# Twelve feed-forward products become eleven, and the shared rotary key moves to the router's product

## What is computed

```python
# feed-forward of each of the two windowed layers, HID = 682
h = layernorm(shift_token(x)) @ w1 + b1          # 256 -> 2 x 682
a, g = split(h, 2)
x = x + (a * gelu(g)) @ w2 + b2                  # 682 -> 256

# latent attention: 16 heads of 16 + 8 rotary columns
c_kv = x @ W_DKV                                 # 256 -> 64
k    = concat(c_kv @ W_UK, rope(x @ W_KR))       # rotary key (8 columns) shared by all heads
# expert layer
logits = x @ gate_w                              # 256 -> 8
```

## Time and profile before

| what | value |
|---|---|
| median of 3 runs | 3233.68 us (3232.84 to 3268.52) |
| the profiled execution | 3231.55 us, its span 3229.8 us |
| PE busy | 2873.4 us, 89% of the span |
| DVE, ACT, POOL busy | 1565.0, 1166.9, 1066.9 us |
| mean granted clock of PE | 0.944 of full speed |
| first block ends, expert block begins | about 2606 us |
| length of a stage with retention, with latent attention | 143.3 us, 167.2 us |

### The profile page before, as it was taken

How to read it: one execution, slowest core, us unless ns; L and a number is a source line. 1 busy time by engine, 2 the same in 40 slices (tenths; PEclk the granted TensorE clock), 3 DMA queues, 4 the chain that set the end, 5 groups by cost and what they waited for, 6 DMA issues and landing times. The chain is left out here.

```text
span 3229.8 us, 41719 instructions
## 1 busy us (share of the span) xinstructions
PE 2873.4 (89%) x15902; PEld 1893.9 (59%) x15902; DVE 1565.0 (48%) x2994; ACT 1166.9 (36%) x2240; POOL 1066.9 (33%) x770
## 2 busy tenths in 40 slices
PE   6999899999989899898999899999988759999990
PEld 3565656556565655545554555555554349989990
DVE  5645456565545556475656565666654410000002
ACT  3444343434343344343444444444432212222221
POOL 4423233342323234252535344443432311111112
PEclk8999999999999999899999999999998679999995
DMA  3000000000001011001010101010101069998874
GB/s 126 10 20 17 24 26 24 14 24 20 17 23 48 21 50 45 14 4 46 4 46 4 47 4 46 4 46 4 40 4 40 2 230 351 349 339 328 324 296 159
DMA packets 86048, 261.69 MB, mean 81 GB/s; under 512 B 10940, under 2 KB 50188, under 8 KB 67164
## 3 DMA queue, kind: packets, MB, share of 16 engines
q1 hardware_dynamic: 79372, 241.26, 20.6%
q0 software_dynamic: 6480, 17.77, 1.4%
HBM read 210.69 MB, written 44.12 MB: 79 GB/s over the span
## 5 line engine op out<-in xcount | busy, mean ns | idle before, releaser
L1171 POOL TENSOR_TENSOR s_qk<-s_qk,s_rrec 128x1024 f32<-128x1024 f32 (+1 forms) x128 | 215.1, 1681 | 761.4 <-DVE s_rrec L1317 761.3
L547 PE MATMUL s_pA<-s_w_wqkv,s_curT 128*128 128x512 f32 x768 | 372.3, 624 | 5.8 <-ACT s_curT L932 3.9
L960 ACT ACTIVATE s_qk<-s_pA,s_mx 128x256 f32<-128x256 f32 (+1 forms) x512 | 221.5, 448 | 420.2 <-DVE s_mx L1313 420.1
L1843 PEld LDWEIGHTS m_ph<-m_xT,m_w 128*128 128x128 f32 x2272 | 267.4, 194 | 5.4 <-issue 1.8
L1843 PE MATMUL m_ph<-m_xT,m_w 128*128 128x128 f32 x2272 | 268.0, 277 | 1.2 <-DVE m_xT L1913 1.2
L1913 DVE COPY m_xT<-m_px 128x256 f32<-128x256 f32 x71 | 30.1, 424 | 476.3 <-PE m_px L1832 476.3
L1857 PE MATMUL m_py<-m_w,m_hT 128*128 128x256 f32 x1136 | 258.1, 381 | 0.0
L547 PEld LDWEIGHTS s_pA<-s_w_wqkv,s_curT 128*128 128x128 f32 x768 | 146.9, 198 | 183.0 <-issue 169.8
L1406 DVE TENSOR_SCALAR s_pairs<-s_pD 128x1024 f32<-128x1024 f32 (+1 forms) x192 | 193.7, 1038 | 105.6 <-PE s_pD L693 67.9
L693 PE MATMUL s_pD<-s_mixer 32*128 32x512 f32 (+3 forms) x1024 | 201.5, 511 | 47.3 <-DVE s_pairs L1406 38.0
L1857 PEld LDWEIGHTS m_py<-m_w,m_hT 128*128 128x128 f32 x1136 | 211.4, 191 | 26.1
(11 more groups left out here) (222 smaller groups left out, 5104.6 us busy)
## 6 DMA issues: line engine op xcount, KB each, us to landing
m_w<-in_m_w SPq DMA_DIRECT2D x142, 1024.0 KB, 5.7
m_xin<-rows_s SPq DMA_DIRECT2D x71, 129.0 KB
m_acc<-acc_s SPq DMA_DIRECT2D x16, 512.0 KB, 5.1
s_cur<-in_x SPq DMA_DIRECT2D x8, 512.0 KB, 3.4
xn_s<-s_cur SPq DMA_DIRECT2D x8, 512.0 KB, 2.6
s_s_tm<-xn_s SPq DMA_DIRECT2D x8, 512.0 KB, 3.2
cur_s<-s_cur SPq DMA_DIRECT2D x8, 512.0 KB, 2.6
s_s<-s_s_tm SPq DMA_DIRECT2D x8, 512.0 KB, 2.6
```

The source lines that it names most:

```text
L547: last = nc.tensor.matmul(out, lhs(c), rhs(c), start=(c == 0), stop=(c == n - 1))
L960: last = nc.scalar.activation(prob[u % 3][:, i * 256 + lo:(i + 1) * 256], ps[:, i * 256 + lo:(i + 1) * 256], ACT.Exp, bias=mx[:, u, i:i + ...
L1171: nc.gpsimd.tensor_tensor(pi, pi, rrec[:, u, :].unsqueeze(2).broadcast_to((P, 4, 256 - lo)), ALU.mult).then_inc(p_rdy, 1)
L1843: last = nc.tensor.matmul(ph[u % 2][:, f * P:(f + 1) * P], w1[:, u % NW, c * F + f * P:c * F + (f + 1) * P], xT[:, u % 2, c * P:(c + 1) * ...
```

## The change

In the feed-forward the chunks are 128 wide, five of them, and the sixth holds what is left, 42 columns. The weights `w1` are laid out anew: chunk by chunk, a then g, and in the last chunk both halves side by side, a at column 0 and g at column 64. So the last chunk is one product of 106 columns in ring D; ACT takes its gelu from ring D's bank (with a semaphore of its own, `last_gelu`), and DVE takes a from the same bank. The memset of the ones waits for this gelu.

For the shared key, the 8 key columns ride with the router's 8 in one product by token (`gw`, 16 columns), which moves ahead of the latent product. DVE rotates them by token with a small table (`lrot`), writes them into `krow` at four heads' places, and PE turns `krow` by four 128x128 transposes in unit 5, behind the value products; DVE copies the result into `KrT`. The product `kr` in its two sets goes, with its weights `lWkr`. POOL clears `krow` once, in stage 8, ahead of its memset of `Vaug`. On DVE the order of unit 4 is now key turn, logits, latents.

```diff
-HCH = 120
+HCH = 128
+LAST_G = 64
+UPW = 2 * HCH * (NHC - 1) + LAST_G + HSZ[-1]
@@ ring_a_jobs
-            if s.here:
+            if s.here and c < NHC - 1:
                 j += [("g", k, c)]
@@ ring_d_jobs
             if s.lat and u == 4:
-                j += [("lat", b), ("kr", b), ("rt", b)]
+                j += [("rt", b), ("lat", b)]
             if s.lat and u == 5:
-                j += head(b, 0)
+                j += [("kr", b)] + head(b, 0)
-WIDE = ("qkT", "S", "qk", "PT", "kr", "lq", "sc", "AT", "ro")
+WIDE = ("qkT", "S", "qk", "PT", "lq", "sc", "AT", "ro")
@@ SP
                 if k == B - 1:
-                    sp.wait_ge(outA, doneA["g", k, NHC - 1])
+                    sp.wait_ge(outA, doneA["g", k, NHC - 2])
@@ PE, up_projection
+                at = 2 * HCH * c
+                if c < NHC - 1:
+                    ps = slotA("g", b, c)
+                    project(ps, lambda k: W["w1"][:, k, at + HCH:at + 2 * HCH], lambda k: zT[:, k, :], DC).then_inc(mmA, 1)
                 ps = slotD("a", b, c)
-                project(ps[0:n, 0:T], lambda k: W["w1"][:, k, c * HCH:c * HCH + n], lambda k: zT[:, k, :], DC).then_inc(mmD, 1)
+                n = HCH if c < NHC - 1 else LAST_G + HSZ[c]
+                project(ps[0:n, 0:T], lambda k: W["w1"][:, k, at:at + n], lambda k: zT[:, k, :], DC).then_inc(mmD, 1)
@@ PE, latent_projections
+                ps = slotD("rt", b)
+                for t in range(NT):
+                    last = project(ps[:, t * (E + LDR):(t + 1) * (E + LDR)], lambda c: x1T[:, c, tile_cols(t)], lambda c: W["gw"][:, c, :], DC)
+                last.then_inc(mmD, 1)
                 ps = slotD("lat", b)
                 project(ps[:, 0:T], lambda c: W["lWd"][:, c, :], xT, DC).then_inc(mmD, 1)
+            def shared_key(b):
+                pe.wait_ge(krow_rdy, b + 1)
                 ps = slotD("kr", b)
-                for i in range(2):
-                    last = project(ps[:, i * T:(i + 1) * T], lambda c: W["lWkr"][:, i, c, :], xT, DC)
-                last.then_inc(mmD, 1)
-                ps = slotD("rt", b)
                 for t in range(NT):
-                    last = project(ps[:, t * E:(t + 1) * E], lambda c: x1T[:, c, tile_cols(t)], lambda c: W["gw"][:, c, :], DC)
+                    last = nc.tensor.transpose(ps[:, tile_cols(t)], krow[:, t].rearrange("p h d -> p (h d)"), ident[:])
                 last.then_inc(mmD, 1)
@@ PE, unit 5
                         latent_values_in(b)
+                        shared_key(b)
                         keys_queries(b, 0)
@@ ACT, gelu
+                at = 0 if c < NHC - 1 else LAST_G
+                if c < NHC - 1:
+                    ps = takeA("g", b, c)
+                else:
+                    act.wait_ge(mmD, DJ["a", b, c] + 1)
+                    ps = pD[:, colsD[DJ["a", b, c]]]
@@ POOL, stage 8
+                        nc.gpsimd.memset(krow, 0.0)
                         nc.gpsimd.memset(Vaug, 0.0).then_inc(vaug_rdy, 1)
@@ DVE, gate_up
-                dve.wait_ge(outA, doneA["g", b, c])
-                if c == NHC - 1:
-                    step(nc.vector.memset(hT[NHC - 1][64:HCH], 1.0))
+                if c < NHC - 1:
+                    dve.wait_ge(outA, doneA["g", b, c])
+                else:
+                    dve.wait_ge(last_gelu, b + 1)
+                    step(nc.vector.memset(hT[NHC - 1][32:64], 1.0))
@@ DVE, key turn (called by router_logits)
+                nc.vector.tensor_tensor(ktmp[:, 0], kr, W["lrot"][:, 0], ALU.mult)
+                for i in range(2):
+                    last = nc.vector.tensor_tensor(turned[:, :, :, i], pairs[:, :, :, 1 - i], sines[:, :, :, i], ALU.mult)
+                step(last)
+                if b == 0:
+                    dve.wait_ge(vaug_rdy, 2)
+                nc.vector.tensor_tensor(krow[:, :, :, LDH:LDH + LDR], ktmp[:, 0].unsqueeze(2).broadcast_to((P, NT, 4, LDR)),
+                                        ktmp[:, 1].unsqueeze(2).broadcast_to((P, NT, 4, LDR)), ALU.add).then_inc(krow_rdy, 1)
@@ DVE, shared_key
-                nc.vector.tensor_tensor(rm[:, 0, :], ps[:, 0:T], W["lcos"], ALU.mult)
-                nc.vector.tensor_tensor(rm[:, 1, :], ps[:, T:2 * T], W["lsin"], ALU.mult).then_inc(outD, 1)
-                dve.wait_ge(outD, doneD["kr", b])
-                step(nc.vector.tensor_tensor(KrT, rm[:, 0, :], rm[:, 1, :], ALU.add))
+                nc.vector.tensor_copy(KrT, ps).then_inc(outD, 1)
@@ DVE, units 4 and 5
                     if s.lat and u == 4:
+                        router_logits(b)
                         latent_in(b)
+                    if s.lat and u == 5:
                         shared_key(b)
-                        router_logits(b)
-                    if s.lat and u == 5:
                         keys_queries(b, 0)
```

More of the change, by code:

```diff
@@ L269, in stream_layers @@
         W["lWqk"] = part(mixer, 9480, 1024, i=2, g=LG, n=P)
-        W["lWkr"] = part(mixer, 10504, 512, i=2, c=DC, n=P)
+        krow = part(mixer, 10504, 512, t=NT, h=4, d=32)
         W["lWo"] = part(mixer, 11016, 512, c=DC, n=D)
@@ L273, in stream_layers @@
         W["lsin"] = part(mixer, 12040, 512)
-        W["gw"] = part(mixer, 12552, 16, c=DC, e=E)
+        W["gw"] = part(mixer, 12552, 32, c=DC, e=E + LDR)
+        W["lrot"] = part(mixer, 12584, 64, i=2, t=NT, d=LDR)
         Ct, St = W["fC"], W["fS"]
@@ L407, in stream_layers @@
         norm_x = sem("norm_x")
+        last_gelu = sem("last_gelu")
         fin_silu = sem("fin_silu")
@@ L1000, in gelu @@
                 n = HSZ[c]
-                ps = takeA("g", b, c)
+                at = 0 if c < NHC - 1 else LAST_G
[4 more added lines that the diff above has]
+                    ps = pD[:, colsD[DJ["a", b, c]]]
                 if b > 0 or c >= 2:
                     act.wait_ge(outD, doneD["a", b, c - 2] if c >= 2 else doneD["a", b - 1, NHC - 1])
-                nc.scalar.activation(gl[c % 2][0:n], ps[0:n, 0:T], ACT.Gelu, bias=W["b1"][0:n, 1, c:c + 1]).then_inc(outA, 1)
+                last = nc.scalar.activation(gl[c % 2][0:n], ps[at:at + n, 0:T], ACT.Gelu, bias=W["b1"][at:at + n, 1, c:c + 1])
+                if c < NHC - 1:
+                    last.then_inc(outA, 1)
+                else:
+                    last.then_inc(last_gelu, 1)
             def final_tanh(b):
@@ L1381, in latent_in, with shared_key_turn @@
                 nc.vector.tensor_copy(latT, ps).then_inc(outD, 1)
+            def shared_key_turn(b):
+                ps = take("rt", b)
+                raw = ps[:, 0:NT * (E + LDR)].rearrange("p (t e) -> p t e", t=NT)
+                kr = raw[:, :, E:E + LDR]
+                pairs = kr.rearrange("p t (d i) -> p t d i", i=2)
+                turned = ktmp[:, 1].rearrange("p t (d i) -> p t d i", i=2)
+                sines = W["lrot"][:, 1].rearrange("p t (d i) -> p t d i", i=2)
+                nc.vector.tensor_tensor(ktmp[:, 0], kr, W["lrot"][:, 0], ALU.mult)
[6 more added lines that the diff above has]
+                                        ktmp[:, 1].unsqueeze(2).broadcast_to((P, NT, 4, LDR)), ALU.add).then_inc(krow_rdy, 1)
+                return raw
             def shared_key(b):
                 ps = take("kr", b)
-                if b:
-                    dve.wait_ge(lq_rdy, LG * b)
-                nc.vector.tensor_tensor(rm[:, 0, :], ps[:, 0:T], W["lcos"], ALU.mult)
-                nc.vector.tensor_tensor(rm[:, 1, :], ps[:, T:2 * T], W["lsin"], ALU.mult).then_inc(outD, 1)
-                dve.wait_ge(outD, doneD["kr", b])
-                step(nc.vector.tensor_tensor(KrT, rm[:, 0, :], rm[:, 1, :], ALU.add))
+                nc.vector.tensor_copy(KrT, ps).then_inc(outD, 1)
             def keys_queries(b, g):
                 ps = take("kc", b, g)
+                if g == 0:
+                    dve.wait_ge(outD, doneD["kr", b])
                 nc.vector.tensor_tensor(KT[:, g % 2, :], ps, KrT, ALU.add).then_inc(outD, 1)
                 ps = take("lq", b, g)
-                if g:
+                if g or b:
                     dve.wait_ge(lq_rdy, LG * b + g)
@@ L1425, in router_logits @@
             def router_logits(b):
-                ps = take("rt", b)
-                lg = ps[:, 0:NT * E].rearrange("p (t e) -> p t e", t=NT)
+                lg = shared_key_turn(b)[:, :, 0:E]
                 step(nc.vector.tensor_reduce(rt1[:, 0], lg, AX.X, ALU.max))
@@ L1969, in tables @@
             "w_lcos": np.tile(lc, (4, 1)).astype(f), "w_lsin": np.tile(ls, (4, 1)).astype(f),
+            "w_lrot": np.stack([by_tile(w[LDH:LDH + LDR].T) for w in (lc, ls)], 1),
             "zrow": np.zeros((1, P), f)}
@@ L1986, in arrange @@
     r["w_ln"] = np.stack([np.stack([per(g), per(b)], 1) for g, b in zip(a["L0_ffn_ln_g"], a["L0_ffn_ln_b"])], 1)
-    r["w_w1"] = np.stack([ch(w) for w in a["L0_ffn_w1"]], 1)
+    w1 = np.zeros((D, DEPTH, UPW), np.float32)
     b1 = np.zeros((HCH, DEPTH, 2, NHC), np.float32)
@@ L1993, in arrange @@
             for i in range(2):
```

(8 more changed lines are left out.)

18 lines of the change are left out of this document (8 added, 10 removed).

## The result

Twenty runs of the changed kernel have a median of 3250.23 us (3240.59 to 3267.59), twenty of the kernel before, on the same chip, 3235.49 us (3221.09 to 3271.14). The ratio is 1.0044, 95% interval [1.0023, 1.0066]: 0.2 to 0.7% slower, where 1.1% faster was forecast. The profiled execution took 3247.42 us, its span is 3245.7, and the forecast was 3198 with a range up to 3222.

A forecast was written before the change was run, and what follows sets the result against it. Up to 2606 us the order of PE's own work was taken to bound the kernel. Gains of 22.0 us (feed-forward) and 11.5 (shared key), 33.5 together, took 3231.55 us to 3198, 1.1% faster; range 3174 to 3222.

The forecast's parts named there:

- The 1.72 us removed, and the wait: Feed-forward end, per stage: one up-projection pair fewer saves 1.72 us; the down-projection then waits some 0.3 us on PE.
- Edits at nothing: Feed-forward: 128 weight columns in five chunks, wider weight loads, SP's wait and PSUM ring changes were taken to cost nothing.
- part 1: Feed-forward in 16 stages: net 1.40 us in 15 and 0.95 in the last, 22.0 us gained, bounds 16 to 27.
- Part 2: Shared key in 8 latent-attention stages: net 1.57 us in seven, 1.0 in the last; 11.5 us gained, bounds 7 to 20.
- the four transposes: Unit 5 of latent stages: turning the key adds 8 records on PE behind the value products, 1.17 us.
- the lost overlap: Unit 5: value and key products no longer run into each other with transposes between them, costing 0.76 us.
- the last stage's bare copy: Last latent stage, without local attention: the latent copy stands uncovered before the values, 0.7 us.
- PE's clock: Low clock stretches each take up to 1.7 us from PE; they would shift, and no row decides whether falls are added.
- rival (b): The clock takes back a part: one more fall in each of 8 latent stages, 13.6 us, giving 3212 us; chance 0.15.
- (c): Slower: added clock falls in all stages cost 54 us against 33.5 gained, giving 3252 us; chance 0.04.
- (d): Comes to nothing: the exponential's chain is the limit and removed work turns into waits, 3231 us; chance 0.06.
- (a): More gain: overlap kept, gelu covered, clock gives back 1 us in 15 stages; 3170 us, some 3180 mid-way; chance 0.2.

The follow-up runs named there:

- run 5: Kernel before with the feed-forward part alone, its last chunk padded to 128 rows and the memset of ones moved early; ratio 0.9916 to the kernel before.
- Run 3: Kernel before with feed-forward chunks of 124 instead of 120, so the last chunk has 63 rows; ratio 1.0085 to the kernel before.
- run 4: Changed kernel with the last chunk's 43 rows filled up to 128 with zero weights; ratio 0.9972 to the kernel before.
- run 7: Changed kernel with 128 rows in the last chunk, early memset, and the key turned before the latent value products; ratio 0.9858 to the kernel before.
- run 10: Kernel before with the key part alone, its four transposes moved ahead of the value products; ratio 0.9986 to the kernel before.
- Run 11: Kernel before with the shared key's products narrowed to 32 columns of tokens from 512, all else the same; ratio 0.9962 to the kernel before.
- run 1: Kernel before with the feed-forward part alone (43 rows in the last chunk), key path as before; ratio 1.0058 to the kernel before.
- Run 9: Kernel before with the feed-forward part alone, last chunk on 128 rows, without the early memset; ratio 0.9950 to the kernel before.
- run 8: Changed kernel with 128 rows, early memset, key turned before the values, and the latent product ahead of the router's; ratio 0.9874 to the kernel before.
- the two parts alone: Kernel before with only the feed-forward part, ratio 1.0058, and with only the key part, ratio 1.0052, each to the kernel before.
- Run 12: Kernel before with the shared key's products made twice, same result and waits; ratio 1.0055 to the kernel before.

## Why the prediction was wrong, point by point

**The 1.72 us removed, and the wait.** Right: 1.72 and 0.43 (0.32 forecast), 2.26 forecast and 2.27 measured in the last stage. The early memset of run 5 removes the wait whole in 15 stages, and brings it from 2.27 to 1.65 us in the last.

**The step that failed first: "Edits at nothing".** It weighed the 128 weight columns of five chunks and took the rows of the sixth as part of the same edit. Run 3 and run 4 show the price of the rows: 1.45 us in each of 16 stages, 23 us, which eats the 22.0 of part 1. I had read the 48 records of the down-projection in the earlier trace rows as one price and not asked what becomes of the short ones among them. The Trainium skill (TensorEngine Tiling (Array Packing), Tiling Modes: Key Properties) says that a change of the tiling mode makes TensorE drain, and (Performance Considerations: When to Use Tiling) it gives a contraction over at most 64 rows to the mode of two row tiles. The trace agrees, with 0.31 us for 0.216 at 43 and at 63 rows and no such step at 83; that these records run in another mode is argued from this, as no row names the mode. The prediction weighed neither that sentence nor the score records at 760.58 us, which showed the step before anything was changed.

**Part 2, the work.** The terms were right in form and too large in unit 5: the four transposes are 4 records and 0.58 us (1855.40 to 1855.98), not 8 and 1.17, and the lost overlap is 1.89 + 1.92 - 2.86 = 0.95 us, not 0.76, together 1.53 for 1.93. Moved ahead of the values (runs 7 and 10) they cost nothing. The turn and the copies on DVE were covered as said, and the last stage's bare copy was 0.78 for 0.7; its 0.88 us for the key's copy was left out.

**"PE's clock", and rival (b): the mechanism was there, its size and its cause were wrong.** The prediction allowed one more fall in each of 8 stages, 13.6 us, at a chance of 0.15, and put it down to transposes in place of dense work; the sum itself had the clock at nothing. The low clock grew by 50 us, some 15 stretches, not 8. Run 11 has no new transposes and shows a growth of 41 us all the same: dense work taken from unit 4 is enough. It is not the only thing that does it, as run 1 grew by 57 us with unit 4 untouched. Up to the first expert product (at 2624.1 us before, 2641.4 after) low clock grew from 284 to 335 us; at 0.42 to 0.5 each that is 21 to 25 us. The bookkeeping to that point: -33.5 forecast, +23.2 the rows, +21 to 25 the clock, +3.0 the longer waits (2.1 ahead of 15 down-projections, 0.88 in the last stage), and -0.4 x 7 = -2.8 for unit 5, which was forecast too dear, together +11 to +15; measured is +17.3. Some 2 to 6 us stay open. One more wait grew, for the exponential ahead of the turned tokens, from 35.9 to 41.1 us over 15 times; no run parts it from the clock. The expert block then gave back 1.4 us, 15.9 in all.

**Of the rivals,** (c) gave 3252 us at a chance of 0.04, nearest to 3250, but for another reason: it had falls in all stages. The changed kernel's first-half stages have one low stretch of 3.4 us each, as before (one has two), and are 0.2 us longer. (d) asked for new waits in place of the removed work: PE's timeline has the 0.43, the two of the last stage and the 5.2 us ahead of the turned tokens: PE is idle for 13 us more in all, not for the 33.5 that (d) needs. (a) is what runs 5 and 7 reach when the two costs are taken away: 3206 and 3187 us, near its 3180, and two of its three assumptions (gelu covered, overlap kept) are just what they establish; the third, that the clock gives back 1 us a stage, they do not show.

**What stays open.** What makes a low stretch start. Run 9 has the same code with and without one by turns, so the moment counts as well as the work, and run 8's order should have mattered and did not. That the two parts alone are each as slow as both together may have this reason; no run here shifts a kernel in time with its work unchanged, which would separate the two.

## What to carry to other kernels

Before re-chunking a contraction, list the row count of every chunk: the odd last one may be cheaper in work and dearer in time, and padding it to full height with zero weights costs nothing (10.63 us for 48 records either way, against 12.00). Put added work of PE ahead of a wait that already exists, not behind it; four transposes went from 1.53 us to nothing by changing places with the group that waits. And where a stage has low stretches of the clock, work taken from PE near one can be worth less than its duration (about half in run 11); price it by a run that narrows the work in place before building the change.

## What the runs showed of the hardware

A full-height float32 record of 256 columns starts 0.216 us after the one ahead; around a pair of 43-row records the four distances are 0.309, 0.320, 0.306, 0.320 us. 63 rows cost the same as 43; 83 cost nothing, and 64-row records among themselves start 0.209 us apart. A low stretch of 3.4 us costs a busy PE 1.6 us (140.7 and 142.3 us in run 9; 4.39 and 6.02 us in unit 5). How long PE's clock stays low changes with the work around, and that can cost as much as the work gives: run 11 removes some 2.7 us per latent stage and has 3.4 to 10.2 us more of low clock in the usual ones, so that some of them (169.2 us) are longer than before (167.2). Run 12 adds 3.5 us and has no more low clock in three of five.
